# Moving the second layer of a fused MLP and its last row to other slots of a hand-written TensorE order

## What is computed

```python
x0 = xk = e                                        # 1024 x 39 x 16
for W in (f0, f1, f2):                             # three layers of the network
    z = einsum('bfd,bgd->bfgd', x0, xk).reshape(b, f * g, d)
    xk = einsum('bpd,pm->bmd', z, W)               # b x 128 x 16
    outs.append(xk)
z = sum(concatenate(outs, axis=1), axis=-1)        # 1024 x 384
h = concatenate([z, dense_ctx], axis=1)            # 1024 x 400
h = maximum(h @ W_top1 + b_top1, 0)                # 512
h = maximum(h @ W_top2 + b_top2, 0)                # 256
y = h @ W_top3                                     # 1
```

## Time and profile before

| | |
|---|---|
| median of 3 runs | 1315.25 us (1313.08 to 1315.68) |
| the profiled execution | 1313.9 us, span from first to last instruction 1312.1 us |
| mean granted TensorE clock | 0.997 |
| TensorE matmul busy | 1262.8 us, 96% |
| weight loads busy | 1022.2 us, 78% |
| VectorE, ScalarE, GpSimd busy | 80%, 71%, 73% |

### The profile page before, as it was taken

One profiled execution on the slowest core, in us unless ns is written; L12 is line 12 of the kernel. 1 busy time (PEld: TensorE's weight loads), 2 busy tenths in 40 slices (PEclk: granted clock), 3 DMA queues, 4 the chain that ended last, 5 costly groups with the idle time before them and its releaser, 6 DMA issues. The chain is left out here.

```text
span 1312.1 us, 21756 instructions
## 1 busy us (share of the span) xinstructions
PE 1262.8 (96%) x5983; PEld 1022.2 (78%) x5983; DVE 1051.5 (80%) x3210; ACT 936.3 (71%) x3084; POOL 953.8 (73%) x743
## 2 busy tenths in 40 slices
PE   3799999999999999999999999999999999999998
PEld 2577778877788777887778878787778877888787
DVE  3598998778977799777997789977898778977783
ACT  2488877667867687677786778866787668767673
POOL 7688888667886688676886768866788668874461
PEclk9899999999999999999999999999999999999999
DMA  5663233332322333213333213333133332321000
GB/s 136 114 174 76 53 58 63 64 63 47 54 58 43 63 65 65 51 23 62 66 65 63 38 33 65 66 63 65 19 55 62 65 63 53 53 56 38 2 2 1
DMA packets 129501, 76.36 MB, mean 58 GB/s; under 512 B 90792, under 2 KB 98201, under 8 KB 129379
## 3 DMA queue, kind: packets, MB, share of 16 engines
q1 hardware_dynamic: 119139, 72.32, 27.1%
q0 software_dynamic: 10240, 2.64, 2.4%
HBM read 68.42 MB, written 3.87 MB: 55 GB/s over the span
## 5 line engine op out<-in xcount | busy, mean ns | idle before, releaser
L414 ACT ACTIVATE parts<-pieces,x_cols 128x128 f32<-128x128 f32 x2560 | 728.6, 372 | 290.4 <-PE pieces L721 239.5
L555 DVE SCALAR_TENSOR_TENSOR parts<-pieces,x_cols,parts 128x128 f32<-128x128 f32 x2432 | 684.3, 343 | 209.2 <-PE pieces L721 171.9
L719 PE MATMUL pieces<-w_hi,cur_hi 128*128 128x512 f32 (+1 forms) x1280 | 542.3, 424 | 6.7 <-DVE parts L555 2.8
L721 PE MATMUL pieces<-w_hi,cur_lo 128*128 128x512 f32 (+1 forms) x1280 | 499.4, 390 | 0.0
L720 PE MATMUL pieces<-w_lo,cur_hi 128*128 128x512 f32 (+1 forms) x1280 | 498.8, 390 | 0.0
L363 POOL TENSOR_TENSOR parts<-parts 128x1024 f32<-128x1024 f32 x127 | 304.1, 2394 | 219.1 <-DVE parts L555 214.0
L354 POOL DMA_INDIRECT emb<-in_table,rows x320 | 311.5, 973 | 81.7 <-issue 67.0
L719 PEld LDWEIGHTS pieces<-w_hi,cur_hi 128*128 128x128 f32 x1280 | 241.4, 189 | 65.8 <-DVE parts L555 9.4
L720 PEld LDWEIGHTS pieces<-w_lo,cur_hi 128*128 128x128 f32 x1280 | 241.9, 189 | 50.0
L721 PEld LDWEIGHTS pieces<-w_hi,cur_lo 128*128 128x128 f32 x1280 | 240.9, 188 | 51.3
L368 POOL TENSOR_TENSOR tails<-parts 128x512 f32<-128x512 f32 x127 | 164.3, 1293 | 18.1
(11 more groups left out here) (78 smaller groups left out, 619.6 us busy)
## 6 DMA issues: line engine op xcount, KB each, us to landing
partners<-x_wide SPq DMA_DIRECT2D x62, 546.0 KB
partners<-x_wide SPq DMA_DIRECT2D x31, 468.0 KB
x_rep<-x_wide SPq DMA_DIRECT2D x96, 78.0 KB
emb<-in_table,rows POOLq DMA_INDIRECT x320
x_diag<-x_cols SPq DMA_DIRECT2D x256, 10.0 KB
x_wide<-emb SPq DMA_DIRECT2D x32, 80.0 KB
x_wide<-emb SPq DMA_DIRECT2D x32, 32.0 KB
wt<-in_wt SPq DMA_DIRECT2D x1, 1024.0 KB
```

The lines of the kernel that those rows point to most:

```text
L414: last = nc.scalar.activation(parts[n % 2][:, 4 * i + r, :], src[:, r * H:(r + 1) * H], ACT.Copy, scale=x_cols[n // 4][:, n % 4, f:f + 1])
L555: nc.vector.scalar_tensor_tensor(acc, src[:, r * H:(r + 1) * H], x_cols[n // 4][:, n % 4, f:f + 1], acc, ALU.mult, ALU.add).then_inc(acc_d ...
L719: nc.tensor.matmul(dst[:, 0:width], hi[:, cols], w1_hi[:, ws], start=True, stop=False)
L721: nc.tensor.matmul(dst[:, 0:width], lo[:, cols], w1_hi[:, ws], start=False, stop=True).then_inc(l2d_ready if q in D_PIECES else l2a_ready, 1)
```

## The change

`top2` goes from slots 86 and 87 to slots 119 and 120, `relu2` from 88 to 122, and `top3` from 119 to 158 (so `copy_y` from 120 to 159). The waits that guard `cur1_bank` follow: before `sum_pairs` of slot 90 for `relu1`, of slot 130 for `relu2`, of slot 10 of the next quad for `copy_y`. `top2` now waits for VectorE's reads of the bank as well. In the tail the warm-up matmuls write `x_bank` in place of `cur1_bank`, and one wait for `copy_y` is added.

```diff
-S_H2 = range(86, 86 + N2 // P)
-S_RELU2 = 88
-S_Y = 119
+S_H2 = range(119, 119 + N2 // P)
+S_RELU2 = 122
+S_Y = 158
...
                 if k == 0:
                     wait(pe, cur1_lo_ready, tile)
                     wait(pe, sum1_ready, tile)
+                    if i == 1:
+                        wait(pe, y_copied, tile // TILES - 1)
                     if i == 2:
                         wait(pe, l3_copied, tile // TILES)
                     if i == 3:
-                        wait(pe, h2_copied, tile // TILES)
+                        wait(pe, h1_copied, tile // TILES * 2)
                     if i == TILES:
-                        wait(pe, y_copied, tile // TILES - 1)
+                        wait(pe, h2_copied, tile // TILES - 1)
...
-            def top2(u, m, sums=h_sums):
+            def top2(u, m, sums=h_sums, tiles=QUADS * TILES):
                 pe.wait_ge(h1_copied, (u + 1) * 2)
+                pe.wait_ge(cur1_lo_ready, tiles)
+                pe.wait_ge(sum1_ready, tiles)
...
-                                top2(u - 1, S_H2.index(at))
+                                top2(u - 1, S_H2.index(at), h_sums, u * TILES + 4)
                             if at == S_Y:
-                                top3(u - 1, u * TILES + 4)
+                                top3(u - 1, min(u * TILES + 5, QUADS * TILES))
...
-            warm_up(4, cur1_bank)
+            warm_up(4, x_bank)
             make_g(u, BLOCKS - 3)
-            warm_up(4, cur1_bank)
+            warm_up(4, x_bank)
...
-            warm_up(5, cur1_bank)
+            warm_up(5, x_bank)
             make_g(u, BLOCKS - 1)
+            pe.wait_ge(y_copied, u)
```

## The result

The changed kernel took 1299.8 us (median of 4 runs, 1298.54 to 1301.78) where the kernel before took 1315.45 (4 runs): a ratio of 0.9889 with a 95% interval of 0.9877 to 0.9901, so 1.1% faster. 1301.4 was forecast, with 1298 to 1306 around it.

The account below looks back on a forecast made before the run. TensorE, busy 96%, was taken to set the pace, so its waits cost time. Per quad 2.73 us added less 4.70 removed gave -1.97, times 7 and 0.15 more: -13.9, from 1315.25 to 1301.4 us, range 1298 to 1306.

Parts of the forecast that it names:

- first half of `top2` and its stall, gone: Slot 86: TensorE's wait for `relu1` and the first half of `top2` disappear, saving 1.94 us per quad.
- second half, gone: Slot 87: the second half of `top2` leaves this place, saving 0.81 us per quad.
- stall in slot 90, gone: Slot 90: `sum_pairs` no longer waits for `relu2`, saving 1.33 us per quad.
- `top3` in slot 119, gone: Slot 119: `top3` leaves this place, saving 0.62 us per quad.
- first half in slot 119: Slot 119: the first half of `top2`, behind VectorE's read of `cur1_bank`, adds 0.94 us per quad; bounds 0.81 and 1.03.
- second half in slot 120: Slot 120: the second half of `top2` adds 0.81 us per quad, up to 0.90 if its waits are exposed.
- `top3` in slot 158: Slot 158: `top3` waits for VectorE's read, delaying the next quad's slot 1 by 0.73 us; bounds 0.66 and 0.85.
- new stall in slot 90: Slot 90: TensorE waits for the bank still held by piece 86, losing 0.25 us per quad; bounds 0 and 0.5.
- Waits exposed: Each `top2` call starts 0.09 us late behind its waits, 1.3 us in all, giving 1302.7 us; chance 0.07.
- The stall comes back, half or whole: Removed TensorE stalls return as bank waits: half in slots 90 to 98, 1308.3 us, chance 0.07; all, 1317 us, 0.05.
- A long wait of `top3`: Slot 158: `top3` waits long for VectorE's read; at 3 us the kernel takes 1322.5 us; chance 0.03.

Follow-up runs that it names:

- e6_sum93: Kernel before, with the first `sum_pairs` of the third tile in a quad with a top moved from slot 90 to 93; quad 155.90 us against 157.30.
- e1_relu1_late: Changed kernel with the second half of `relu1` moved on ScalarE from slot 84 to slot 87; quad 155.10 us against 155.33.
- e2: Changed kernel with `top3` in slot 159 instead of 158 and `copy_y` in slot 0 of the next quad; quad 154.76 us against 155.33.
- e4: Changed kernel with the three waits before each half of `top2` issued four times, 18 more per quad; quad 155.68 us against 155.33.
- e3: Changed kernel with `relu2` moved on ScalarE from slot 122 to slot 128; quad 157.84 us against 155.33.
- e7: Kernel before, with `top2` two slots later (slots 88 and 89) and `relu2` in slot 90; quad 156.90 us against 157.30.

## Why the prediction was right

**The sum, term by term, per quad.**

| term | forecast | measured |
|---|---|---|
| first half of `top2` and its stall, gone | -1.94 | gone: no wait for L469 in the loop |
| second half, gone | -0.81 | gone |
| stall in slot 90, gone | -1.33 | -1.33 (e6_sum93, slots 90 to 93; -1.40 by its quad) |
| `top3` in slot 119, gone | -0.62 | gone |
| first half in slot 119 | +0.94 | +0.93 |
| second half in slot 120 | +0.81 | +0.81 |
| `top3` in slot 158 | +0.73 | +0.80 |
| new stall in slot 90 | +0.25 | +0.26, and 0.25 by e1_relu1_late (slots 89 and 90) |
| all | -1.97 | -1.97 |

Each of the places was read off the timeline before and stands where it was said. The two terms that could go wrong were the new ones. For the stall in slot 90 the reading was that ScalarE is late by its relu and the bank four slots on feels it; e1 shows that by moving that relu alone. For slot 158 it was that VectorE's read ends 0.4 us after TensorE asks, and that 0.3 us of a wait one slot further is used up in exchange; e2 shows that by going one slot on. `top3` started 0.14 us behind the read, where I took 0.07 and gave 0.19 as the bound; that is the 0.07 by which this term was too small. The mechanism is shown, but the agreement of the whole to the last digit is luck: this term was off by 0.07, and two profiles of one kernel differ by 0.08.

**What the sum left out.** A piece that follows 128x128 products takes 0.78 to 0.80 us and not 0.70 (311.54 to 312.33 after; 281.01 to 281.79); that is the 0.17 by which slots 86 to 88 gave more than forecast. This is missing from the costs of what goes and of what comes; it cancels, since such places are as many as before: slots 87, 88 and, behind `top3`, 120 have it before; 120, 121 and, behind `top3`, 159 after.

**From the quad to the median.** 13.9 us were forecast, the medians differ by 15.65. That is inside the interval of the ratio (13.0 to 16.2 us). The two profiled executions separate loop and startup: quad 1 starts at 191.0 us before and at 192.9 after, and from there to the end it takes 1121.1 and 1107.1 us, 14.0 less. The whole executions differ by only 12.1 (1313.9 and 1301.78), and the 1300.0 that the prediction named beside that execution was missed by 1.8, because the startup happened to take 1.9 us more. By the clock in the stretches from 44 to 80 us 1.8 of it can be the clock: the kernel before lost 16 x 0.21 = 3.4 us of full clock there. On the chip where both kernels ran again the medians differ by 14.2 (1311.33 and 1297.17). So no term accounts for the 1.6 us by which the forecast of 1301.4 was too high; a startup that moves by 4 us between executions of one kernel can make such a difference of medians of four, but of the executions that were not profiled the startup isn't known.

**The rivals.** *Waits exposed* (1): the live price of the added waits is small, `top2` in slot 119 starts 0.05 us after it could; e4 shows 0.04 us for a wait in that place and nothing in the slot after. *The stall comes back, half or whole* (2, 3): refuted by e6 for the stall in slot 90, and for both by the slots: outside the places of the table none is longer than before by more than 0.03 us. With it falls, for this kernel, the reading that I took from the Trainium skill (Perfetto Trace Analysis, Identifying the Most-Contended Engine), where TensorE's headroom is judged by MFU (its arithmetic as a share of the peak) or by weight-load busy time. Weight loads are busy 78%, VectorE 80%, yet every microsecond that TensorE no longer waited was gained whole. The trace does not agree with taking the higher of these two as the engine that sets the pace. I did not work out the MFU, so this speaks of the weight-load share alone. *A long wait of `top3`* (4): 0.4 us, with no drift.

**Where I was wrong** was in the experiments: e3's 0.7 us, since I left out the split ahead of `relu2` and its wait for VectorE; e7's 0.7 in place of 0.40, since I counted the wait to the relu's end and not to TensorE's start; and the startup, which moved by 4.2 us and not by 2.

## What to carry to other kernels

Where one engine sets the pace in a written-out order, read starts, not ends, find the places where a start comes later than the pitch allows, and cost a move as what stands there with its stall, against the same work elsewhere with the wait that is live there; the quad then came out within what two profiles of one kernel differ by (0.1 us). A chain of product, relu, product, relu through one bank wants its links in different free stretches of the bank: two slots further in the same stretch only moves the stall to the next user. Before a producer is put late, ask not only how far its reader is but which waits stand ahead of it on its own engine: two slots were the difference between nothing and 2.2 us. And a stall of some 2 us can cost more than its length: in two of the thirteen quads that had one in e3 and e7 the clock fell right behind it, for another 1.5 to 1.6 us.

## What was not expected of the hardware

A satisfied wait on TensorE costs 0.04 us (in the loop) to 0.07 us (in the tail) when it stands behind a wait that is released late, and nothing when matmuls are still to be worked off.

TensorE's clock fell to its lower level behind single stalls of 1.9 us in an otherwise full stream, in 2 of 13 cases, and within 1.5 us of the restart; behind the stalls of 1.0 and 1.3 us of the kernel before it never fell in the loop. What decides between the two cases was not found out.

The startup of one kernel, with the same instructions and the same data, took 4.3 us more in one execution than in the other, with a granted clock of 0.70 against 0.89 in the stretch from 44 to 60 us; differences below that are better read from the quads than from the whole.
